# One core, a block with attention: the second half's V products of the last head pair, one query tile at a time

## The reference

```python
q, k, v = (xn @ w + b for each)            # (heads, 1024, 64), then rope on q and k
scores = einsum('bhqd,bhkd->bhqk', q, k) / 8
attn = softmax(where(causal, scores, -inf))
ctx = einsum('bhqk,bhkd->bhqd', attn, v)   # the V products
attn_out = ctx @ o_w + o_b + xn
```

## Time and profile before

| | us |
|---|---|
| median of 3 runs (2492.89 to 2502.37) | 2493.31 |
| profiled execution, its own time | 2495.71 |
| its span | 2493.8 |
| PE busy in the span | 1981.7 (79%) |
| DVE, ACT, POOL busy | 1655.0, 1438.5, 855.7 |
| granted TensorE clock, mean over the span | 0.914 of full |

### The profile page before, as it was taken

The page is one execution under the profiler, slowest core; times in us unless marked ns, Lnnn a source line. Parts: engine busy times, 40 slices in busy tenths (PEclk is TensorE's granted clock), DMA queues, the critical chain, the costliest instruction groups (busy, mean ns, idle before and its releaser), DMA issues.

```text
span 2493.8 us, 41045 instructions
## 1 busy us (share of the span) xinstructions
PE 1981.7 (79%) x9942; PEld 1292.0 (52%) x9942; DVE 1655.0 (66%) x2947; ACT 1438.5 (58%) x2785; POOL 855.7 (34%) x797
## 2 busy tenths in 40 slices
PE   3738999879773999987966499996996659999698
PEld 1226666547323666655732366664662246666466
DVE  4946676669485666657948566665794756666488
ACT  3516676647452767655744367674674336766366
POOL 1534233133163433403315434331332453343132
PEclk9869999979796999998979699998896979999899
DMA  2011111001001110101100111100100011110011
GB/s 60 0 32 39 31 27 36 1 28 40 10 0 40 31 39 20 35 1 32 36 10 0 51 25 33 32 23 9 31 28 10 12 39 33 26 38 17 10 36 32
DMA packets 65391, 64.33 MB, mean 26 GB/s; under 512 B 12184, under 2 KB 48384, under 8 KB 65280
## 3 DMA queue, kind: packets, MB, share of 16 engines
q1 hardware_dynamic: 65280, 63.01, 9.6%
HBM read 27.31 MB, written 2.10 MB: 12 GB/s over the span
## 4 chain that ended last, share of the span: by engine, by line
PE 52%; DVE 18%; ACT 12%; issue 11%; POOL 3%; ACTq 1%; SPq 1%; DMA 1%; DVEq 1%; POOLq 0%
PE ps L1380 9%; PE ps L1219 6%; PE ps L1221 6%; PE ps L1220 6%; DVE state L959 6%; PE ps L1369 5%; PE ps L1359 4%; ACT probs L724 4%; PE ps L1360 3%; PE ps L1344 2%; PE ps L1486 2%; PE ps L1395 2%; ACT probsT L736 2%; ACT k_high L717 2%; PE ps L1247 2%
## 5 line engine op out<-in xcount | busy, mean ns | idle before, releaser
L736 ACT ACTIVATE probsT<-ps 128x512 f32<-128x512 f32 (+3 forms) x768 | 349.3, 492 | 361.8 <-PE ps L1369 361.8
L1359 PE MATMUL ps<-k_high,q_split 128*128 128x512 f32 (+3 forms) x768 | 312.3, 407 | 133.4 <-DVE q_split L1027 68.3
L724 ACT ACTIVATE probs<-ps,least 128x640 f32<-128x640 f32 (+7 forms) x512 | 380.3, 743 | 53.5 <-DVE least L1037 46.6
L1369 PE MATMUL ps<-ident,probs 128*128 128x128 f32 x2304 | 350.4, 279 | 10.3 <-ACT probsT L736 10.1
L1369 PEld LDWEIGHTS ps<-ident,probs 128*128 128x128 f32 x2304 | 261.8, 141 | 130.6 <-issue 93.0
L1380 PE MATMUL ps<-probsT,vals 128*64 128x512 f32 (+3 forms) x1536 | 292.6, 505 | 21.1 <-ACT probsT L736 21.1
L1044 DVE TENSOR_REDUCE least<-ps 128x1 f32<-128x640 f32 (+3 forms) x256 | 262.2, 1024 | 8.8
L1360 PE MATMUL ps<-k_low,q_split 128*128 128x512 f32 (+3 forms) x768 | 261.2, 352 | 0.0
L1359 PEld LDWEIGHTS ps<-k_high,q_split 128*128 128x128 f32 x768 | 150.1, 195 | 192.2 <-ACT probs L724 110.7
L562 POOL TENSOR_TENSOR roped<-turned,roped 128x512 f32<-128x512 f32 x128 | 163.0, 1274 | 236.8 <-DMA roped<-turned 195.5
L1037 DVE CUSTOM_DVE_ANT_0 ps<-ps,row_masks 128x128 f32<-128x128 f32 (+3 forms) x256 | 127.0, 496 | 166.5 <-PE ps L1360 163.6
(11 more groups left out here) (213 smaller groups left out, 3968.7 us busy)
## 6 DMA issues: line engine op xcount, KB each, us to landing
roped<-turned SPq DMA_DIRECT2D x512, 64.0 KB, 2.0
w<-in_w SPq DMA_DIRECT2D x128, 128.0 KB, 2.0
w_pair<-in_w_pairs SPq DMA_DIRECT2D x36, 128.0 KB, 2.6
xin<-in_x SPq DMA_DIRECT2D x5, 512.0 KB, 3.9
out<-acc SPq DMA_DIRECT2D x4, 512.0 KB, 3.8
pos<-in_c_pos SPq DMA_DIRECT2D x1, 512.0 KB, 4.8
v_w<-in_v_w SPq DMA_DIRECT2D x1, 512.0 KB
o_w<-in_o_w SPq DMA_DIRECT2D x1, 512.0 KB
```

Source lines behind the costliest of these rows:

```text
L724: act.activation(probs[:, t % 2, 0:width(t)], banks(2 * (t % 2))[:, 0:width(t)], ACT.Exp, bias=least[:, t:t + 1], scale=-1.0, accum_out=ro ...
L736: act.activation(dst, ps[:, T_BANK + g % 2, 0:k1 - k0], ACT.Copy).then_inc(t_taken, 1)
L1359: pe.matmul(o, q, k_high[par][h][:, k0:k1], start=True, stop=False)
L1369: made = pe.transpose(ps[:, T_BANK + g % 2, at - k0:at - k0 + P], probs[:, t % 2, at:at + P], ident[:, :])
```

## The change

In the last step of a batch the second half's V products are no longer made key tile by key tile after all transposes, but query tile by query tile: tiles 4 and 5 at t = 14 after the transposes of unit 13, tile 6 at t = 15 after those of unit 14, and tile 7 at the end. The new `weigh_tile` multiplies 128 columns at a time, for key tiles 0 to i and both heads. It waits for the copies of its own query tile, and at the first tile for the bank. The transposes of the inverses (`spread_inverses`) now stand ahead of tile 7 instead of behind all products. The other steps are as they were. `pv_out` is raised by two for each tile, so that four tiles count as the eight key tiles did.

```diff
+TILE_AT = {14: (4, 5), 15: (6,)}
...
+                def weigh_tile(n, par, i):
+                    if i == TPH:
+                        pe.wait_ge(ctx_ready, 2 * n + 1 + 1)
+                    pe.wait_ge(t_taken, GROUPS * n + group_at(2 * i + 1) + 2 + 2)
+                    at = P * (i - TPH)
+                    for j in range(i + 1):
+                        for g in range(2):
+                            made = pe.matmul(ps[HD * g:HD * (g + 1), CTX_BANK, at:at + P], vals[par][:, j, g, :],
+                                             probsT[1][:, g, PT_STEP[1] * (i - TPH) + j, :], start=(j == 0), stop=(j == i),
+                                             skip_group_check=True)
+                    made.then_inc(pv_out, TILES // TPH)
...
                         elif not last:
                             scores(n + 1, 1 - par, t + 2 - UNITS_A)
+                        if last and t in TILE_AT:
+                            for i in TILE_AT[t]:
+                                weigh_tile(n, par, i)
...
                 turn_probs(n, UNITS_A - 1)
-                weigh_values(n, 1, 1, tuple(range(TILES)))
                 bank_free(X_ALL - 2)
                 spread_inverses(n, 1)
+                weigh_tile(n, 1, TILES - 1)
                 bank_free(X_ALL - 1)
                 output(n, PAIRS - 1, 1)
```

## The result

The changed kernel takes 2493.08 us (median of 20 runs, 2485.66 to 2498.06). The kernel before, over 20 runs, takes 2499.11 us (2492.89 to 2504.14); the median of 2493.31 that the prediction started from was that of the first three of them and lies near the low end of this range. The ratio is 0.9977, interval 0.9968 to 0.9987: a real gain of 5.7 us (3.2 to 8.0), where 9.1 was forecast. The time lies 1.1 us above the stated range.

A forecast was written before the change was run, and what follows sets the result against it. PE was taken to bound the kernel (79% busy), with a chain without slack at each batch's attention end. There 5.08 us gained less 2.80 of delay gave 2.28 a batch, 9.1 in four: 2493.31 to 2484.2 us, range 2475 to 2492.

The forecast's parts named there:

- Columns and prices: Last step's V products on PE: 13312 columns as before, 0.415 ns each, 0.16 us for coming from full-width instructions.
- Rival 1: In `weigh_tile`, narrow 128-column products cost above 0.150 us per two instructions; 2496 midway, 2508 at the upper bound; chance 0.12.
- The delay: Early tiles make the transposes of units 14 and 15 late; PE released at 500.73 against 497.93, a 2.80 us loss.
- The cover of the inverses: ACT's copy and tile 7 hide the inverses' transposes and ACT's `factors`, which cost 1.2 us before.
- Four batches give 9.1 us: The 2.28 us saved at each batch's attention end, over four batches, takes the median from 2493.31 to 2484.2.
- The local 2.28: At one batch's attention end: 7.15 us behind the release become 2.07, a gain of 5.08, less 2.80 of delay.
- rival 2: After each attention, moved work meets the clock's fall and rise badly; 5.7 of 9.1 us gone, 2489.9; chance 0.14.
- two kinds of batch: DVE's last multiplications 617.18, 611.55 and 617.26 us apart: kinds 5.7 us apart, only by where the clock falls and rises.
- The base: The starting median of the kernel before, 2493.31 us, from which the forecast took 9.1 us.

The follow-up runs named there:

- the one with four additions: The changed kernel with four DVE additions into buffers nobody reads yet, right behind the barrier after attention in each batch; ratio 0.9992 to the kernel before.
- the kernel with one query tile: The changed kernel without the last pair's V products for query tiles 4, 5 and 6, tile 7 behind the inverses; 2476.73 us, ratio 0.9919.
- that with two: The changed kernel without the last pair's V products for query tiles 4 and 5, tiles 6 and 7 behind the inverses; 2471.98 us, ratio 0.9896.
- the filled one with one tile early: The changed kernel with only tile 4 early, tiles 5 to 7 behind the inverses, and ten constant PE products behind the attention; ratio 0.9939.

## Why the prediction was right at the place and wrong in the total

- **Columns and prices: right.** 0.415 ns per column and 0.16 us for coming to the products gave 2.50, 1.65 and 1.99 us; 2.55, 1.68 and 1.99 were measured. Rival 1 (narrow products are dear) is out: 44 in a row ran at 2.55 / 22 = 0.116 us per two with the change of shape in it, not at 0.150 or more. With that the Trainium skill's figure for a stream of weight load and matmul ("TensorE: Matmul & The Clock Gate", section "Back-to-back issue gap", 81 ns each at 128 columns) doesn't bind 64-column products of two heads, which came 58 ns apart.
- **The delay: right.** 2.80 us of later release were forecast. From unit 13's transposes to the start of tile 7 it is 502.63 - 494.68 = 7.95 us, against 497.93 - 492.85 = 5.08 before, 2.87 later; and 2.01 us follow in place of 7.15.
- **The cover of the inverses: right.** Split off, their move is worth 1.29 us of the 2.27, the tiles 0.97.
- **The failed step: "Four batches give 9.1 us".** The local 2.28 was right to 0.01, the multiplication by four was not: 5.7 us arrived. It holds only if all that was not changed takes as long as before, and this term was put at nothing. Over three distances the unchanged parts took 4.15 us more (0.87, 0.79, 1.43 and 1.15, less 0.1), and 2.65 of 6.8 us were left. I had the mechanism as rival 2, with a chance of 0.14, and read from the earlier trace rows that two kinds of batch exist; but I took it as an accident that might or might not come, and not as something that shapes every change of a batch's length. The runs show that it does: no proportion between -1.0, -1.3, -2.3, -2.4, -3.9 and -5.1 us of place and the times. The rival's own sum comes near: three long batches, each less its 2.28 us, would be 614.9 us apart, and 613.94, 614.36 and 615.04 were measured; it had 5.7 us gone where 4.15 went in these distances.
- **The base.** 2493.31 was the median of three runs with 2502.37 among them; twenty runs give 2499.11. With that base the forecast would have been 2490.0, and the time inside a range of the same width; but that would have been luck, for the ratio forecast, 2484.2 / 2493.31 = 0.9963, lies outside the measured interval (0.9968 to 0.9987) whatever the base. The range's upper end, 2492, allowed for almost no error of the base, though the three runs were 9.5 us apart, as much as the whole gain. A slip besides: a quarter of rival 1's 0.12 is 0.03 above 2505.8, not 0.04.

What is shown: the place saves what the sum says; the total doesn't follow the place, and can go against it; the lost time sits in unchanged parts in which the granted clock changes, and it went in the middle batch, which was of the short kind before. What was only argued: that a batch's length draws to certain values, 614.4 in five of the kernels, and as the mean of a long and a short distance in the kernel before and the one with four additions, 607.5 in two others; four other kernels have distances that fit neither (611.66, 617.33, 610.32 and 610.78). What decides which kind a batch becomes, its length or the moment at which the execution began, stays open. I did not find a reading of the rows from which these values could have been forecast.

## What to carry to other kernels

In a kernel whose TensorE clock falls and rises in every pass of its outer loop, a saving of some us per pass has no fixed worth: compare the length of passes in the profile first, and where they alternate without reason in the code, give a small saving a wide range: here the places gave 9.1 us and 5.7 arrived, and in another kernel they gave 3.9 and 9.7 arrived. Filling PE's stalls with work that nobody waits for can be worth more than shortening the chain (1.0% here, against 0.23%), but at one place alone it may bring nothing. And three runs are no base for a forecast finer than their own spread.

## What the runs showed of the hardware

- Less work can be slower: the kernel with one query tile took 4.75 us more than that with two, and 30 us more of its span ran at 1.2 GHz.
- The same kernel, the filled one with one tile early, took 2470.50 us at a granted clock of 0.927 and 2497.29 at 0.916.
- The same 75 instructions of PE were busy for 26.52 us at a granted clock of 0.76, and for 28.70 at 0.69.
- fp32 products with weights 64 wide, for two heads in turn and 128 columns each, ran 44, 60 and 84 in a row at 56 to 58 ns per instruction, with a weight load for each; full-width ones took 111 ns.
- The clock's share of the time is large: 431 us before and 462 after, of some 2493, ran at 1.2 GHz, and the fillers that left 184 of the 431 made the kernel 1.0% faster (0.9900, 0.9885 to 0.9915), with 55 filler products a batch.
